# Sums of 32 steps' outputs on TensorE by products with the identity, and GpSimd in the recurrence from pair 53

## The chip, the core and the metric

One core of a Trainium2 chip. The metric is the device time of one launch in microseconds; three runs of the kernel before gave 1234.92, 1235.33 and 1239.51 us.

## What is computed

A layer norm of x (8 x 512 x 256) feeds two branches, a recurrent attention and a mixture of experts, whose product is added to x:

```python
def step(S, inp):                      # 512 steps; S is [batch, head, 16, 16], 8 batches x 16 heads
    qt, kt, vt, at, gkt = inp
    S = S * jnp.exp(gkt)[..., None]
    sab = jnp.einsum('bhk,bhkv->bhv', at, S)
    S = S + kt[..., None] * (sab[..., None, :] + vt[..., None, :])
    ot = jnp.einsum('bhk,bhkv->bhv', qt, S)
    return (S, ot)
...
xn = _layernorm(x, axis=-1)
s = attention(xn)                      # the recurrence, its output gated, normed and times Wo
g = _silu(experts(xn))                 # 8 experts, the 2 best of each token, gelu, layer norm
x = x + s * g
```

## The kernel before

**Layout.** The 128 pairs of batch and head are the 128 partitions, so a state is 16 x 16 values on each partition, and the 512 steps are done one after the other, two at a time. The program calls two steps g a pair; there are 256 pairs (g from 0 to 255), eight to a chunk (NP = 8), 32 chunks. Each chunk's records (decay, key, query, value, output gate, the a of the reference) are in memory as one block of 768 KB and are loaded by SyncE into one of three buffers of rbh; the load of chunk c + 3 waits for the gating of chunk c.

**Stages.** First TensorE projects 32 tiles of tokens and VectorE turns them into records, woven into pairs 0 to 28. At pair 29 VectorE does the routing. GpSimd then issues 64 scatters (L499) that sort the tokens by expert, and when all have landed ScalarE loads the first sorted rows (L698). Then TensorE and ScalarE run 39 expert tiles of 256 rows each: turn the rows (L875), first product (L887), gelu (L708), second product in two halves (L899, with the bias in L901), scaling of each half by ScalarE (L719). Last, the expert outputs are loaded, added, normed, and multiplied with the attention's output; this stage is woven into the recurrence from pair 224 (WOVEN = 28 chunks) and needs GpSimd's spreads (L533 to L538).

**One pair on VectorE alone.** Up to pair 55 `two_steps` does all on VectorE: products of the state with a (L1167), the decayed state (L1170), sums (L1172), the new state (L1190, L1196), and the reading of outputs. Reading is a product with q over 16 x 16 values (`read_left` L318 for the state that the pair before left, `read_found` L323 for the state in the middle) written to prod_q, with a 17th column, and a sum over the 17 columns (`sum_row`, L1156) two pairs later, into obh. Output row r is 2g - 1 + side. Every 16 rows are multiplied by the output gate (`gate_outputs`, L300) at the fourth pair (GATED = 3) of the next chunk.

**One pair shared.** From pair 56 (chunk SHARED = 7) `two_shared_steps` leaves the big products to GpSimd (`products`: L312 for a and decay, L329 for the reading; L318 and L323 at the first pair of a chunk), with a and two small tiles in PSUM. VectorE keeps the sums, the outer products and the state (L1206 to L1227). GpSimd's program for these pairs is one list in order: the products of a pair, then, at fixed pairs, the landing of an expert tile's half (`land`, L527, an indirect DMA that waits for ScalarE's scaled half), the numbering of the next tile (`number`, L517), gating and preparation of chunks, and from pair 224 the outputs' work. The pairs for landings come from a plan: landing of tile t's first half when (g - 56) x 3.83 + 390 is at least 390 + 15.9 t. An engine executes its instructions in order, so what waits holds back all behind it.

**Order of the names.** s_chain counts VectorE's steps in a pair (nine each), s_q the readings, s_o the summed rows, s_og the gated chunks, s_ys the scaled halves. TensorE's expert part starts with `turn_rows(0, 0, 0)`, which waits for the first sorted rows. The region `work` holds records first and expert tiles later.

## Time and profile before

| | |
|---|---|
| median of three runs | 1235.33 us |
| the profiled execution | 1241.86 us, span 1240.1 us |
| busy: TensorE, VectorE, GpSimd, ScalarE | 76%, 90%, 75%, 32% |
| pairs on VectorE alone, with tiles | 0 to 28 |
| routing | about 240 to 260 us |
| scatters on GpSimd | 260 to 362 us |
| first expert tile on TensorE | 366 us |
| pair 56, first with GpSimd | 391 us |
| last expert tile's end | 1003 us |

The page gives busy time by engine, the chain of work that ended last, and groups of instructions by line. The timeline gives start and duration of each instruction and, in brackets, how long its engine was idle before it and what ended that. VectorE's instructions overlap a little at their ends, so the distance between two starts says more than a duration.

### The profile page before, as it was taken

To read this page: it belongs to the slowest core of one execution; us is meant where nothing else is said; L and a number is where in the kernel's file an instruction comes from. 1 tells how busy PE (TensorE), PEld (TensorE's weight loads), DVE (VectorE), ACT (ScalarE), POOL (GpSimd) and SP (SyncE) were. 2 spreads that over 40 slices of the span, in tenths; PEclk is the share of its full clock that TensorE was granted. 3 is DMA by queue.
4 is the path that set the end of the run, shared out by engine and by line. 5 is a ranking of instruction groups with operands and counts; after the bars stand their busy time and mean duration, and the time that the engine had idled before them with its cause. 6 is when DMAs were issued, how large, how long until landed. Compare 5 with 4: busy or idle time off the path is not lost.

```text
span 1240.1 us, 17339 instructions
## 1 busy us (share of the span) xinstructions
PE 941.8 (76%) x3773; PEld 686.6 (55%) x3774; DVE 1122.2 (90%) x3478; ACT 398.0 (32%) x1015; POOL 933.0 (75%) x926
## 2 busy tenths in 40 slices
PE   5888888200019999999999999999999952667663
PEld 2333333100017778888787878887888841445442
DVE  3789999999999999999999999899999999978882
ACT  3444544200003232233223333332332213454552
POOL 3766666447753888888888888888888888777763
PEclk9788989655559999999999999999999985676777
DMA  5565655464333566666566666666666453443322
GB/s 163 171 226 178 188 201 190 147 211 114 108 107 119 174 190 200 195 199 189 181 188 192 199 201 185 185 192 199 199 199 192 131 150 101 111 135 117 83 68 56
DMA packets 238034, 202.59 MB, mean 163 GB/s; under 512 B 140401, under 2 KB 216017, under 8 KB 237969
## 3 DMA queue, kind: packets, MB, share of 16 engines
q1 hardware_dynamic: 160930, 82.81, 25.5%
q10 hardware_dynamic: 70224, 100.49, 24.4%
q0 software_dynamic: 6816, 18.69, 4.5%
q14 instruction: 54, 0.44, 0.1%
q8 instruction: 10, 0.16, 0.1%
HBM read 139.42 MB, written 62.54 MB: 163 GB/s over the span
## 4 chain that ended last, share of the span: by engine, by line
PE 56%; DVE 17%; POOL 8%; DMA 7%; issue 6%; ACT 4%; SPq 3%; ACTq 0%; DVEq 0%; POOLq 0%
PE psF L899 22%; PE psA L887 20%; POOL xs_d L499 6%; PE psA L955 4%; PE psF L901 4%; DMA rec_d<-work 3%; PE psF L917 2%; DMA work<-xs_d 2%; DVE obh L1156 2%; SPq L337 2%; DVE ubuf L1172 1%; PE psT L875 1%; DVE prod_a L1167 1%; DVE work L1009 1%; PE psT L949 1%
## 5 line engine op out<-in xcount | busy, mean ns | idle before, releaser
L312 POOL TENSOR_TENSOR prod_a<-state,rbh 128x512 f32<-128x512 f32 x200 | 254.4, 1272 | 94.0 <-DVE state L1227 68.8
L899 PE MATMUL psF<-wts,work 128*128 128x256 f32 x1248 | 290.0, 386 | 2.3 <-ACT work L708 1.2
L887 PE MATMUL psA<-xT,wts 128*128 128x256 f32 x1248 | 281.9, 385 | 1.3 <-ACT xT L702 0.8
L887 PEld LDWEIGHTS psA<-xT,wts 128*128 128x128 f32 x1248 | 235.6, 191 | 45.0 <-issue 13.8
L899 PEld LDWEIGHTS psF<-wts,work 128*128 128x128 f32 x1248 | 232.3, 191 | 48.1 <-issue 16.8
L329 POOL TENSOR_TENSOR prod_q<-state,rbh 128x512 f32<-128x512 f32 x175 | 221.9, 1268 | 0.0
L1156 DVE TENSOR_REDUCE obh<-prod_q 128x16 f32<-128x272 f32 x512 | 218.7, 428 | 0.0
L708 ACT ACTIVATE work<-psA,b_sb 128x256 f32<-128x256 f32 x312 | 130.7, 470 | 162.4 <-PE psA L887 159.0
L1214 DVE TENSOR_REDUCE ubuf<-prod_a 128x16 f32<-128x272 f32 x200 | 86.1, 431 | 46.5 <-POOL prod_a L312 46.4
L719 ACT ACTIVATE work<-psF,work 128x256 f32<-128x256 f32 x78 | 36.9, 473 | 256.8 <-PE psF L901 245.7
L875 PE MATMUL psT<-ident,work 128*128 128x128 f32 x156 | 24.2, 279 | 118.2 <-DMA work<-xs_d 118.2
L481 POOL TENSOR_TENSOR rinv<-ssm,neghalf 128x16 f32<-128x16 f32 x32 | 100.7, 3148 | 2.7
L499 POOL DMA_INDIRECT xs_d<-x_acc,idx x64 | 79.0, 1234 | 19.5 <-issue 18.9
L527 POOL DMA_INDIRECT y_d<-work,ids x78 | 78.9, 1011 | 14.6 <-issue 12.6
L1227 DVE TENSOR_TENSOR state<-psB,outer 128x256 f32<-128x256 f32 x200 | 84.4, 422 | 5.8
L1206 DVE TENSOR_TENSOR prod_a<-state,psT 128x256 f32<-128x256 f32 x200 | 83.9, 420 | 6.0
L875 PEld LDWEIGHTS psT<-ident,work 128*128 128x128 f32 x156 | 19.3, 143 | 123.9 <-issue 115.3
L1209 DVE TENSOR_REDUCE psB<-prod_a 128x16 f32<-128x272 f32 x200 | 86.8, 434 | 0.0
L1220 DVE TENSOR_TENSOR psB<-prod_a,psB 128x256 f32<-128x256 f32 x200 | 83.8, 419 | 0.0
L1212 DVE TENSOR_TENSOR psB<-rbh,psB 128x256 f32<-128x256 f32 x200 | 83.7, 419 | 0.0
L1222 DVE TENSOR_TENSOR outer<-rbh,psB 128x256 f32<-128x256 f32 x200 | 83.0, 415 | 0.0
L841 PE MATMUL psA<-w_kq,xT 128*128 128x512 f32 x128 | 78.9, 749 | 0.0
(171 smaller groups left out, 1564.0 us busy)
## 6 DMA issues: line engine op xcount, KB each, us to landing
wts<-in_L_ffn_W_dram ACTq DMA_DIRECT2D x78, 1024.0 KB, 5.4
rec_d<-work SPq DMA_DIRECT2D x32, 768.0 KB
rbh<-rec_d SPq DMA_DIRECT2D x32, 768.0 KB, 5.6
xs_d<-zero SPq DMA_DIRECT2D x26, 387.0 KB, 9.2
work<-xs_d ACTq DMA_DIRECT2D x39, 258.0 KB, 5.6
wts<-y_d ACTq DMA_DIRECT2D x16, 512.0 KB, 5.7
x_acc<-in_L_attn_x_dram SPq DMA_DIRECT2D x32, 128.0 KB
o_d<-obh SPq DMA_DIRECT2D x32, 128.0 KB, 7.3
```

Of the source, the lines that this page charges most:

```text
L312: eng.tensor_tensor(prod_a[:, n, 1:3, :, 0:HD], state[:, g % SR, :, :].unsqueeze(1).broadcast_to(wide), rows.unsqueeze(2).broadcast_to(wid ...
L329: eng.tensor_tensor(prod_q[:, g % SR, :, :, 0:HD], state[:, g % SR, :, :].unsqueeze(1).broadcast_to(wide), rbh[:, u, 2 * n - 1:2 * n + 1, ...
L481: pool.tensor_tensor(rinv[:, u, :], ssm[:, u, :], neghalf[:, 0:H], ALU.pow).then_inc(s_ng, 1)
L499: pool.indirect_dma_start(xs_d, bass.IndirectOffsetOnAxis(idx[:, 2 * n + c:2 * n + c + 1], 0), x_acc[:, n, :], None).then_inc(s_sc, 16)
L708: act.activation(hT[:, m, :], psA[m // 2 % 2][:, m % 2 * MT:(m % 2 + 1) * MT], ACT.Gelu, bias=b1_sb[:, bass.ds(e * FC + m, 1)]).then_inc(s ...
L887: mm = pe.matmul(psA[m // 2 % 2][:, m % 2 * MT:(m % 2 + 1) * MT], w1_sb[v][:, c, m * P:(m + 1) * P], xgT[:, c, :], start=(c == 0), stop=(c ...
L899: pe.matmul(psF[q][:, 0:D], hT[:, m, q * P:(q + 1) * P], w2_sb[v][:, m, :], start=(m == 0), stop=False)
L1156: dve.tensor_reduce(obh[:, c % OB, row % RING, :], prod_q[:, g % SR, side, :, :], AX.X, ALU.add).then_inc(s_o, 1)
L1206: dve.tensor_tensor(prod_a[:, n, 0, :, 0:HD], old, over_v(home_a[:, n, :]), ALU.mult).then_inc(s_chain, 1)
L1209: dve.tensor_reduce(u1, prod_a[:, n, 0, :, :], AX.X, ALU.add).then_inc(s_chain, 1)
L1214: dve.tensor_reduce(raw, prod_a[:, n, 2, :, :], AX.X, ALU.add).then_inc(s_chain, 1)
L1227: dve.tensor_tensor(new, home_o, outer[:, 1, :, :], ALU.add).then_inc(s_chain, 1)
```

## The change

Five things are changed together.

1. For pairs 32 to 47 the readings go to a ring of 16 rows, `q_rows`, in the upper part of `work` (the records there are done by then), and VectorE's sums of rows 64 to 94 are left out. Instead TensorE adds the 17 columns of eight rows at a time in PSUM: 17 products of the identity with one column of each row (128 columns with a step of 17 elements), in four groups of four pairs. VectorE fills the padding column once at pair 32 and waits for the groups (s_ro) before it uses ring rows again.
2. The gating of chunks 4 and 5 reads PSUM and moves from the fourth to the seventh pair (LATER = 6) of the next chunk: pairs 46 and 54. A last row of chunk 5 is gated by an instruction of its own. The gating of chunk 6, at pair 59, stays.
3. In pairs 34 to 49 `read_found` moves behind the new state, to where the sum stood.
4. GpSimd joins at pair 53 (SWITCH) in place of 56. It no longer waits for its scatters' completion (ScalarE still does), numbers tile 0 behind pair 56 and lands tile 0's first half at pair 57 in place of 56. Chunk 6's preparation also copies a to PSUM.
5. TensorE does the four groups ahead of its expert tiles, and waits for the gating of chunk 5, at pair 54, before it touches the first tile, because both use the same PSUM bank.

```diff
--- before.py
+++ after.py
@@ -46,7 +46,11 @@
 SR = 4
 RB = 3
 GATED = 3
+LATER = 6
 SHARED = 7
+SWITCH = 53
+SUMS = 32, 48
+SUMMED = range(2 * SUMS[0], 2 * SUMS[1] - 1)
 LAND0, LAND_STEP = 390.0, 15.9
 PAIR_STEP = 3.83
 
@@ -162,9 +166,12 @@
         psT = [ps(f"psT{n}", [P, 512]) for n in range(2)]
         sums = [psF[0], psF[1]]
         home_a = psT[1][:, 0:NP * HD].rearrange("p (n k) -> p n k", n=NP)
+
+        q_sums = psF[0][:, :].rearrange("p (r v) -> p r v", v=HD)
         home_u = psB[1][:, 0:4 * HD].rearrange("p (r j v) -> p r j v", r=2, j=2)
         home_o = psB[1][:, 4 * HD:4 * HD + HD * HD].rearrange("p (v k) -> p v k", v=HD)
 
+        q_rows = work[:, 32 * D - RING * HD * ROW:32 * D].rearrange("p (r v k) -> p r v k", r=RING, v=HD)
         oTs = xTs
         sel = gw[:, 0, :, :].rearrange("p t e -> p (t e)")
         b2_flat = b2_sb[:, :, :].rearrange("a e n -> a (e n)")
@@ -247,6 +254,7 @@
         s_dec = sem("s_dec")
         s_q = sem("s_q")
         s_pad = sem("s_pad")
+        s_ro = sem("s_ro")
         s_o = sem("s_o")
         s_og = sem("s_og")
         s_od = [sem(f"s_od{n}") for n in range(OB)]
@@ -291,14 +299,31 @@
 
         def prepared(c):
 
-            return 8 * min(c + 1, SHARED + 1) + (c >= SHARED) + 3 * max(0, c - SHARED)
+            return 8 * min(c + 1, SHARED + 1) + (c >= SHARED - 1) + (c >= SHARED) + 3 * max(0, c - SHARED)
 
         def shared(g):
-            return g // NP >= SHARED
+            return g >= SWITCH
+
+        def read_rows(g):
+
+            if SUMS[0] <= g < SUMS[1]:
+                return q_rows[:, 2 * g % RING:2 * g % RING + 2, :, :]
+            return prod_q[:, g % SR, :, :, :]
+
+        def summed(row):
+
+            return row + 1 - max(0, min(row + 1 - SUMMED.start, len(SUMMED)))
 
         def gate_outputs(eng, c):
-            eng.tensor_tensor(obh[:, c % OB, :, :], obh[:, c % OB, :, :], rbh[:, c % RB, :, O_:O_ + HD], ALU.mult)\
-                .then_inc(s_og, 1)
+            given = max(0, min(RING, SUMMED.stop - c * RING)) if SUMMED.start <= c * RING else 0
+            if given > 0:
+                at = c * RING - 2 * SUMS[0] + 1
+                ins = eng.tensor_tensor(obh[:, c % OB, 0:given, :], q_sums[:, at:at + given, :],
+                                        rbh[:, c % RB, 0:given, O_:O_ + HD], ALU.mult)
+            if given < RING:
+                ins = eng.tensor_tensor(obh[:, c % OB, given:, :], obh[:, c % OB, given:, :],
+                                        rbh[:, c % RB, given:, O_:O_ + HD], ALU.mult)
+            ins.then_inc(s_og, 1)
 
         def over_v(row):
             return row.unsqueeze(1).broadcast_to([P, HD, HD])
@@ -315,12 +340,12 @@
 
         def read_left(eng, g):
             n, u = (g - 1) % NP, (g - 1) // NP % RB
-            eng.tensor_tensor(prod_q[:, g % SR, 0, :, 0:HD], state[:, g % SR, :, :],
+            eng.tensor_tensor(read_rows(g)[:, 0, :, 0:HD], state[:, g % SR, :, :],
                               over_v(rbh[:, u, 2 * n + 1, Q_:Q_ + HD]), ALU.mult).then_inc(s_q, 1)
 
         def read_found(eng, g):
             n, u = g % NP, g // NP % RB
-            eng.tensor_tensor(prod_q[:, g % SR, 1, :, 0:HD], state[:, g % SR, :, :],
+            eng.tensor_tensor(read_rows(g)[:, 1, :, 0:HD], state[:, g % SR, :, :],
                               over_v(rbh[:, u, 2 * n, Q_:Q_ + HD]), ALU.mult).then_inc(s_q, 1)
 
         def read_both(eng, g):
@@ -507,7 +532,6 @@
             pool.wait_ge(s_idx, 3)
             for n in range(NT):
                 scatter(n, 1)
-            pool.wait_ge(s_sc, 32 * NT)
 
             def number(t):
                 v = t % 2
@@ -540,12 +564,14 @@
             def products(g):
                 c, n = g // NP, g % NP
                 pool.wait_ge(s_chain, g * CHAIN + 1)
+                if g == SWITCH:
+                    pool.wait_ge(s_prep, prepared(c))
                 if n == 0 and c == SHARED:
                     pool.wait_ge(s_prep, prepared(c))
                 if n == 0 and c > SHARED:
                     pool.wait_ge(s_pp, 3 * (c - SHARED))
                 decay_and_read(pool, g)
-                pool.wait_ge(s_o, 2 * (g - SR) + 1)
+                pool.wait_ge(s_o, summed(2 * (g - SR)))
                 if n == 0:
                     read_left(pool, g)
                     read_found(pool, g)
@@ -584,12 +610,13 @@
                     pool.wait_ge(s_pp, done + 2)
                     pool.tensor_tensor(fk, fk, both(REC + F_), ALU.mult).then_inc(s_pp, 1)
 
-            number(0)
             landed = 0
-            for g in range(SHARED * NP, T // 2):
+            for g in range(SWITCH, T // 2):
                 products(g)
+                if g == SHARED * NP:
+                    number(0)
                 ready = LAND0 + landed // MH * LAND_STEP
-                if landed < NM * MH and (g - SHARED * NP) * PAIR_STEP + LAND0 >= ready or g >= WOVEN * NP - 1:
+                if landed < NM * MH and g > SHARED * NP and (g - SHARED * NP) * PAIR_STEP + LAND0 >= ready or g >= WOVEN * NP - 1:
                     while landed < NM * MH:
                         t, q = divmod(landed, MH)
                         land(t, q)
@@ -599,9 +626,9 @@
                         if g < WOVEN * NP - 1:
                             break
                 if g % NP == GATED and g // NP > SHARED:
-                    pool.wait_ge(s_o, g // NP * RING)
+                    pool.wait_ge(s_o, summed(g // NP * RING - 1))
                     gate_outputs(pool, g // NP - 1)
-                if 4 <= g % NP < 7 and g // NP + 1 < NCH:
+                if 4 <= g % NP < 7 and SHARED < g // NP + 1 < NCH:
                     prepare_part(g // NP + 1, g % NP - 4)
                 s = g - WOVEN * NP
                 if s >= 0:
@@ -901,6 +928,20 @@
                     pe.matmul(psF[q][:, 0:D], ones[0:1, :], b2_flat[:, bass.ds(e * D, D)], start=False, stop=True)\
                         .then_inc(s_y, 1)
 
+
+            for m in range(SUMS[0] // 4, SUMS[1] // 4):
+                at = (4 * m - SUMS[0]) * 2
+                pe.wait_ge(s_chain, (4 * m + 4) * CHAIN + 1)
+                pe.wait_ge(s_q, 2 * (4 * m + 3) + 1)
+                for c in range(SHARED - 1):
+                    if SUMS[0] < (c + 1) * NP and (c + 1) * NP + LATER < 4 * m + 4 and SUMMED.stop > c * RING:
+                        pe.wait_ge(s_og, c + 1)
+                for k in range(ROW):
+                    mm = pe.matmul(q_sums[:, at:at + NP, :], ident[:, :], q_rows[:, 8 * m % RING:8 * m % RING + NP, :, k],
+                                   start=(k == 0), stop=(k == ROW - 1))
+                mm.then_inc(s_ro, 1)
+            pe.wait_ge(s_og, (SUMMED.stop - 1) // RING + 1)
+
             turn_rows(0, 0, 0)
             with pe.Fori(0, (NM - 1) // 2) as tp:
                 for v in range(2):
@@ -1129,7 +1170,7 @@
                 dve.tensor_reduce(pair[:, :, :], cross[:, :, :, :], AX.X, ALU.add).then_inc(s_prep, 1)
                 dve.wait_ge(s_prep, first + 6)
                 dve.tensor_tensor(f1, f1, f2_, ALU.mult).then_inc(s_prep, 1)
-                if c >= SHARED:
+                if c >= SHARED - 1:
                     dve.tensor_copy(home_a, a1).then_inc(s_prep, 1)
                 dve.wait_ge(s_prep, prepared(c))
 
@@ -1148,12 +1189,14 @@
             def sum_row(g, side):
 
                 row = 2 * g - 1 + side
+                if row in SUMMED:
+                    return
                 c = row // RING
                 dve.wait_ge(s_q, min(2 * g + 1, T))
                 dve.wait_ge(s_chain, min(g + 1, T // 2) * CHAIN)
                 if row % RING == 0 and c >= OB:
                     dve.wait_ge(s_od[c % OB], c // OB * 16)
-                dve.tensor_reduce(obh[:, c % OB, row % RING, :], prod_q[:, g % SR, side, :, :], AX.X, ALU.add).then_inc(s_o, 1)
+                dve.tensor_reduce(obh[:, c % OB, row % RING, :], read_rows(g)[:, side, :, :], AX.X, ALU.add).then_inc(s_o, 1)
 
             def two_steps(g, tile=None):
                 n, u, par = g % NP, g // NP % RB, g % 2
@@ -1168,6 +1211,8 @@
                                   rbh[:, u, 2 * n:2 * n + 2, A_:A_ + HD].unsqueeze(2).broadcast_to([P, 2, HD, HD]),
                                   ALU.mult).then_inc(s_chain, 1)
                 dve.tensor_tensor(decayed, old, over_v(rbh[:, u, 2 * n, F_:F_ + HD]), ALU.mult).then_inc(s_dec, 1)
+                if SUMS[0] + NP <= g < SUMS[1] and g % 4 == 0:
+                    dve.wait_ge(s_ro, (g - NP - SUMS[0]) // 4 + 1)
                 dve.wait_ge(s_chain, done + 1)
                 dve.tensor_reduce(ubuf[:, par, :, :], prod_a[:, n, 0:3:2, :, :], AX.X, ALU.add).then_inc(s_chain, 1)
                 if g > 0:
@@ -1188,12 +1233,15 @@
                 dve.wait_ge(s_chain, done + 4)
                 dve.wait_ge(s_dec, g + 1)
                 dve.tensor_tensor(decayed, decayed, outer[:, 0, :, :], ALU.add).then_inc(s_chain, 1)
-                read_found(dve, g)
-                dve.tensor_scalar(prod_q[:, g % SR, 1, :, HD], u1, pair[:, 0, n:n + 1], None, ALU.mult).then_inc(s_chain, 1)
+                if g - 2 not in range(*SUMS):
+                    read_found(dve, g)
+                dve.tensor_scalar(read_rows(g)[:, 1, :, HD], u1, pair[:, 0, n:n + 1], None, ALU.mult).then_inc(s_chain, 1)
                 if tile is not None:
                     scale_a(tile - 1)
                 dve.wait_ge(s_chain, done + 6)
                 dve.tensor_tensor(new, decayed, outer[:, 1, :, :], ALU.add).then_inc(s_chain, 2)
+                if g - 2 in range(*SUMS):
+                    read_found(dve, g)
                 if g > 1:
                     sum_row(g - 2, 1)
 
@@ -1233,7 +1281,7 @@
 
             def chunk(c, u, slots=None, outs=None):
                 dve.wait_ge(s_rb[u], c // RB * 16 + 16)
-                if c == SHARED:
+                if c == SHARED - 1:
                     dve.wait_ge(s_v, NT)
                     dve.wait_ge(s_gam, NT)
                 if c <= SHARED:
@@ -1243,9 +1291,16 @@
                 for n in range(NP):
                     if slots is not None and slots + n == NT + 1:
                         route()
-                    if n == GATED and 0 < c <= SHARED:
-                        dve.wait_ge(s_o, c * RING)
+                    if 0 < c <= SHARED and n == (LATER if (c - 1) * RING in SUMMED else GATED):
+                        dve.wait_ge(s_o, summed(c * RING - 1))
+                        if (c - 1) * RING in SUMMED:
+                            dve.wait_ge(s_ro, (min(c * RING, SUMMED.stop) - SUMMED.start) // NP + 1)
                         gate_outputs(dve, c - 1)
+                    if c * NP + n == SUMS[0]:
+                        for r in range(RS):
+                            dve.wait_ge(s_recd[r], 16 * (NT // RS))
+                        dve.memset(q_rows[:, 0::2, :, HD], 0.0).then_inc(s_pad, 1)
+                        dve.wait_ge(s_pad, SR + 1)
                     if shared(c * NP + n):
                         two_shared_steps(c * NP + n, outs + n if outs is not None else None)
                     else:
@@ -1275,7 +1330,7 @@
                 for side in range(2):
                     sum_row(g, side)
             sum_row(T // 2, 0)
-            dve.wait_ge(s_o, NCH * RING)
+            dve.wait_ge(s_o, summed(NCH * RING - 1))
             gate_outputs(dve, NCH - 1)
 
             for n in range((NCH - WOVEN) * NP - LAG, NT - 1):
```

## Rows read from the trace of the kernel before

**Rows 1.** The page: busy time by engine, chain that ended last, chunk loads.

```profile
PE 941.8 (76%) x3773; PEld 686.6 (55%) x3774; DVE 1122.2 (90%) x3478; ACT 398.0 (32%) x1015; POOL 933.0 (75%) x926
...
PE 56%; DVE 17%; POOL 8%; DMA 7%; issue 6%; ACT 4%; SPq 3%; ACTq 0%; DVEq 0%; POOLq 0%
...
rbh<-rec_d SPq DMA_DIRECT2D x32, 768.0 KB, 5.6
```

**Rows 2.** Timeline, TensorE: start, duration, work, [idle before, its end].

```profile
366.11 1.09 PE L875 MATMUL psT<-ident,work 128*128 128x128 f32 x4 [114.60 <-DMA work<-xs_d]
```

**Rows 3.** Windows: length; busy PE, PEld, DVE, ACT, POOL; PEclk, DMA, GB/s.

```profile
391.00:1005.00 614.00, 606.65 (x2713) 490.56 (x2711) 578.35 (x1818) 183.95 (x414) 540.33 (x534) 1.00 0.62 186
```

**Rows 4.** Timeline of ScalarE, behind the expert stage.

```profile
1039.07 1.02 ACT L772 ACTIVATE wts<-psF,ysh,yrs 128x256 f32<-128x256 f32 x2 [19.89 <-POOL ysh L538]
```

**Rows 5.** Timelines of ScalarE and GpSimd: results and landings, tiles 0 and 38.

```profile
382.32 0.47 ACT L719 ACTIVATE work<-psF,work 128x256 f32<-128x256 f32 x1 [2.55 <-PE psF L901]
...
394.04 1.01 POOL L527 DMA_INDIRECT y_d<-work,ids  x1 [0.15 <-issue]
...
999.26 0.47 ACT L719 ACTIVATE work<-psF,work 128x256 f32<-128x256 f32 x1 [3.14 <-PE psF L901]
...
1000.80 1.01 POOL L527 DMA_INDIRECT y_d<-work,ids  x1 [0.16 <-issue]
```

**Rows 6.** Timeline of GpSimd, a landing in between.

```profile
782.38 1.02 POOL L527 DMA_INDIRECT y_d<-work,ids  x1 [1.41 <-issue]
```

**Rows 7.** Timeline of VectorE, a pair that it does alone.

```profile
264.25 0.68 DVE L1167 TENSOR_TENSOR prod_a<-state,rbh 128x512 f32<-128x512 f32 x1
...
268.79 0.69 DVE L1167 TENSOR_TENSOR prod_a<-state,rbh 128x512 f32<-128x512 f32 x1
...
270.68 0.43 DVE L1156 TENSOR_REDUCE obh<-prod_q 128x16 f32<-128x272 f32 x1
271.03 0.23 DVE L1178 SCALAR_TENSOR_TENSOR ubuf<-ubuf,pair 128x16 f32<-128x16 f32 x1
```

**Rows 8.** Timeline of VectorE, padding columns filled at the start.

```profile
48.36 0.15 DVE L1267 MEMSET prod_q<- 128x16 f32 x4
```

**Rows 9.** Timeline of VectorE: pair 53; chunk 7 prepared; pairs 56 and 57.

```profile
375.43 0.69 DVE L1167 TENSOR_TENSOR prod_a<-state,rbh 128x512 f32<-128x512 f32 x1
...
389.05 0.30 DVE L1122 TENSOR_TENSOR cross<-rbh 128x128 f32<-128x128 f32 x1
...
390.79 0.31 DVE L1133 COPY psT<-rbh 128x128 f32<-128x128 f32 x1
391.13 0.42 DVE L1206 TENSOR_TENSOR prod_a<-state,psT 128x256 f32<-128x256 f32 x1
...
394.69 0.42 DVE L1206 TENSOR_TENSOR prod_a<-state,psT 128x256 f32<-128x256 f32 x1
```

**Rows 10.** Timeline of GpSimd, the last scatter.

```profile
360.35 1.22 POOL L499 DMA_INDIRECT xs_d<-x_acc,idx  x1 [0.30 <-issue]
```

**Rows 11.** Timeline of TensorE: tile 0, its transposes; four transposes later.

```profile
367.95 5.56 PE L887 MATMUL psA<-xT,wts 128*128 128x256 f32 x16 [0.76 <-ACT xT L702]
374.04 3.72 PE L887 MATMUL psA<-xT,wts 128*128 128x256 f32 x16 [0.53 <-ACT work L708]
377.60 0.60 PE L875 MATMUL psT<-ident,work 128*128 128x128 f32 x4
...
1044.49 1.11 PE L939 MATMUL psB<-ident,gT 128*128 128x128 f32 x4 [3.23 <-ACT gT L780]
```

**Rows 12.** Timeline of queues and TensorE around tile 2's wait for rows.

```profile
402.42 0.36 SPq L371 DMA_DIRECT2D rbh<-rec_d  x1
...
403.04 0.69 ACTq L698 DMA_DIRECT2D work<-xs_d  x1
...
412.23 0.73 PE L875 MATMUL psT<-ident,work 128*128 128x128 f32 x4 [2.67 <-DMA work<-xs_d]
...
413.18 5.14 PE L899 MATMUL psF<-wts,work 128*128 128x256 f32 x16 [0.23 <-issue]
```

## What the change does to the time, predicted

> **What bounds the kernel now.** I read the page first, then the waits, then the order of time around the two places where engines meet. VectorE is busy for 90% of the span and TensorE for 76% [rows 1], which reads like a kernel bound by VectorE. The chain that ended last says something else: 56% of it is TensorE and 17% VectorE [rows 1]. The stages explain it. Up to 366.11 us TensorE has been idle for 114.60 us [rows 2], while VectorE works and GpSimd issues scatters. From 391 to 1005 us TensorE is busy for 606.65 of 614 us at full clock: this is the expert stage, 39 tiles [rows 3]. After it TensorE and ScalarE wait again, for 19.89 us, until GpSimd's spread of the first outputs, which its list of work puts at pair 224 of the recurrence [rows 4].
>
> So two tracks run beside each other: the expert tiles (TensorE, ScalarE) and the recurrence (VectorE, GpSimd). They are tied by GpSimd's landings of tile results (line 527), which stand at fixed pairs in its program and wait for ScalarE's scaled result (line 719). I compared the two for the same tile. Tile 0: result done at 382.79 us, landing at 394.04, so 11.1 us in hand (less the 0.15 us of issue). Tile 38, the last: 999.73 and 1000.80, so 0.9 us [rows 5]. In between GpSimd already waits for a tile here and there, 1.41 us at 782.38 [rows 6]. That is the main reading: at the start the recurrence is the later of the two, at the end they are level. A recurrence that comes earlier buys at most 0.9 us at tile 38 unless the tiles come earlier too.
>
> **The change part by part, in time of the profiled execution.** It ran 1241.86 us with a span of 1240.1; the three timed runs have a median of 1235.33, so this profile is 6.5 us above it. I add what I find to both.
>
> *The removed sums.* 31 rows (64 to 94) lose their VectorE sum. One sum takes 0.43 us but its neighbour starts 0.35 us after it (270.68 to 271.03) [rows 7], 0.34 elsewhere; with 0.345 that is 31 x 0.345 = 10.7 us. A pair of 4.54 us (264.25 to 268.79) becomes 3.86. The product of line 323 moves behind the new state, where the sum stood, so an instruction of about the same length still lies between the state and its first reader; I cost the move at nothing. Were that cover gone, a pair would wait for up to those 0.34 us and the sum would have saved nothing.
>
> *Small additions on VectorE.* One memset of the padding with its wait: the nearest row is four memsets of 128x16 in 0.15 us each [rows 8]; bounds 0.1 and 0.6 us, I take 0.3. The wait beside it is for the last records in memory; the program finishes them at pair 28, four pairs and the routing earlier, and a transfer of the same 768 KB lands in 5.6 us [rows 1], so it costs nothing. The copy of line 1133 now also in chunk 6: 0.34 us (390.79 to 391.13) [rows 9]. The gate of chunk 4 only moves; that of chunk 5 moves behind pair 53, so 0.34 us less ahead of it.
>
> *GpSimd from pair 53.* Pair 53 starts at 375.43 now [rows 9], so after the change at 375.43 - 10.7 + 0.3 + 0.34 - 0.34 = 365.0 us. The last scatter is issued at 360.35 for 1.22 us [rows 10], so GpSimd is free, by 3.5 us. Shared pairs start 3.56 us apart when nothing is added (391.13 to 394.69) [rows 9], against 4.54: 3.0 us gained over three pairs. The gate at pair 54, in two parts, costs 0.34 + 0.2, of which 0.34 was there before. Chunk 7 is prepared at 376.2 instead of 389.05 [rows 9]: **the recurrence leads by 12.8 us** when the expert stage begins.
>
> *TensorE's sums.* Four groups of 17 products with 128 columns; in float32 each shows as two instructions (32 for a tile's 16 calls), so 34 a group. The trace shows no product with a moving operand that takes every 17th element. The nearest rows are four transposes of 128 columns: 1.11 us at 1044.49, in a stretch of low clock, and 0.60 at full clock (377.60) [rows 11]; less the first one's fill that is 0.25 and 0.11 us an instruction. A group costs 8.5 us or 3.8 us. After idling, tile 0 ran 16 instructions in 5.56 us and the next 16 in 3.72 [rows 11], so the clock should rise inside a group: about 22 instructions in 5.5 us and 12 in 1.3, 6.8 us. I take 6.8. It is hidden as long as a group ends before its reader: the third group can start at pair 44 and its reader, the gate of chunk 4, stands at pair 46, two pairs or 7.7 us later, 7.5 with the signals. The ring of rows needs a group only every four pairs, 15.4 us.
>
> *The new wait ahead of the tiles.* This is the term that decides. TensorE now waits for the gate of chunk 5, at pair 54: 365.0 + 3.56 = 368.5, plus 0.6 for the gate: 369.2 us. Before, it started at 366.11, when the first rows had landed [rows 2]. Queued behind this wait is everything TensorE has: all 39 tiles. **Tiles start 3.1 us later.** Bounds: 0 if the pairs shrink by more than I think, 5 if the groups run at low clock throughout and the copies or waits cost their upper ends.
>
> *Moved numbering and landing.* The first numbering goes behind pair 56, about 382 us; the load that needs it is issued behind tile 0's second half, after its first half's result at 386, so it is hidden. The first landing goes from pair 56 to 57, one pair of 3.7 us later. SP's loads of chunks 7 and 8 follow gates that come at pairs 46 and 54: needed at 56 and 60, they have about 37 and 22 us for a load of 5.6 us [rows 1].
>
> *Sum.* Relative to the tiles the recurrence is now 12.8 + 3.1 = 15.9 us earlier, 12.2 at tile 0. Tile 0 had 11.1 in hand: GpSimd waits 1 us there already, and as the hand falls to 0.9 us at tile 38 it waits 15.0 us in all. The products of the recurrence stand behind each such wait, so the lead is given back. Tile 38 lands at its result, 3.1 us later than now, which was 0.9 before its landing: +2.2 us. After it nothing changes. Span 1240.1 + 2.2 = 1242.3; against the median, 1235.33 + 2.2, **1237.5 us**.
>
> **The rivals.** *R1, the tiles also speed up.* In tile 2 TensorE waited 2.67 us for the next rows, whose load was issued at 403.04, 0.6 us after SP's chunk load of 402.42; its next 16 products then took 5.14 us [rows 12], where 16 take 3.72 at full clock [rows 11]: 4.1 us lost. The phase between gates and tiles changes, so this may go: 1237.5 - 4.1 = 1233.4, and down to 1229 if smaller delays go too. Against it: chunks and tiles differ in length, drift through each other in any case and meet elsewhere.
>
> *R2, the landings don't hold the recurrence.* If it keeps its 12.8 us to pair 224, the time is 1222.5. For it: ScalarE stands ready for 19.89 us there [rows 4]. Against: [rows 5, 6].
>
> *R3, slower: a group outlasts its reader.* If a group takes 15 us (34 x 0.44, a strided operand that costs nearly twice the 0.25 us, for which there is no row), the gate at pair 46 waits 15.0 - 7.5 = 7.5 us, the gate at 54 moves by as much and with it all tiles: 1237.5 + 7.5 = 1245.0. It decides from 7.5 us a group on. The Trainium skill speaks for it ("SBUF - State Buffer", section "Door 1: The DMA port swizzle"): float32 reads stepping over more than four elements leave the 16-byte line each time and pay. By that rule the group would be the long one; no row of this trace shows such an operand on TensorE, and the page gives no size.
>
> *R4, the freed VectorE time is lost.* If taking a sum out uncovers waits, a pair stays at 4.2 us instead of 3.86, tiles start 5.4 us later still: 1242.9. Against: each waiting instruction has one independent instruction left ahead of it.
>
> **How the numbers follow.** Forecast 0.50 (its own range 1234 to 1241, from the bounds 0 and 5 of the start and the spread of the three runs), R1 0.22, R2 0.07, R3 0.12, R4 0.09. This kernel's runs can tell about 0.5%, 6.2 us: faster means below 1229.2, slower above 1241.5. Faster: R2 and a third of R1 with everything small gone, 0.15. Slower: R3, two thirds of R4 and the upper tail of the forecast, 0.21. The same: 0.64. The range 1229 to 1245 leaves out R2, the part of R1 below 1229 and about half of R3, 0.19 in all.
>
> **What would show it.** Right: pairs 36 to 48 about 3.86 us apart; TensorE's first transpose of rows near 369.2 us, right behind line 300's second part; landings with waits ahead of them that sum to about 15 us; the last landing about 3 us later than its result now. Wrong: first tile at or before 366 (then +2.2 becomes -0.9), groups on TensorE longer than 7.5 us, landings that follow pairs rather than results, or a stretch from the first to the last tile that differs from now by more than 2 us, which moves everything behind it.

## Result: 2% slower, and the profile after

The changed kernel takes 1261.77 us (median of four runs, 1261.2 to 1262.31), the kernel before 1235.12 on the same chip: ratio 1.02 [1.018, 1.0219]. The forecast was 1237.5 with a range of 1229 to 1245. One run of the kernel before that took 2013.68 us, on a chip of the experiments (chip 0), stands outside all ratios below. The profiled run took 1261.2 us with a span of 1259.5; below, times of before are those of its own profile, span 1240.1.

The page of the changed kernel: busy time by engine, share of the chain that ended last, scatters as a group (count, busy us, mean ns, idle before).

```profile
PE 968.5 (77%) x3909; PEld 713.2 (57%) x3910; DVE 1109.4 (88%) x3444; ACT 397.9 (32%) x1015; POOL 930.0 (74%) x932
...
PE 47%; DVE 27%; POOL 7%; issue 7%; ACT 4%; DMA 3%; another core or an unknown queue 2%; SPq 1%; ACTq 0%; DVEq 0%; POOLq 0%
...
L524 POOL DMA_INDIRECT xs_d<-x_acc,idx x64 | 69.8, 1090 | 19.5 <-issue 18.9 <-POOL idx L520 0.3 <-POOL x_acc L531 0.3
```

VectorE is busy 12.8 us less than in [rows 1] (31 sums at 0.43 us are 13.3), so the work did leave it, and the kernel is slower all the same. The new entry in the chain is "another core or an unknown queue", 2% or some 22 us. One core runs, so it is a wait whose releaser the profile doesn't know. The waits (engine, line, waited for: total, times, longest) and the timeline of VectorE name it:

```profile
DVE obh L321 <- remote: 21.9, 1, 21.9
```

```profile
329.66 0.69 DVE L1210 TENSOR_TENSOR prod_a<-state,rbh 128x512 f32<-128x512 f32 x1
...
333.24 0.42 DVE L348 TENSOR_TENSOR work<-state,rbh 128x256 f32<-128x256 f32 x1
355.56 0.42 DVE L321 TENSOR_TENSOR obh<-psF,rbh 128x256 f32<-128x256 f32 x1 [21.89 <-remote]
```

The waiting instruction is the gate of chunk 4 at pair 46. Between 333.66 and 355.56 us VectorE does nothing. It waits for the third group of TensorE's sums (s_ro at 3). TensorE's timeline has the four groups and the first expert tile:

```profile
292.66 8.03 PE L940 MATMUL psF<-work,ident 128*128 128x128 f32 x34 [41.86 <-DVE work L348]
308.33 8.02 PE L940 MATMUL psF<-work,ident 128*128 128x128 f32 x34 [7.64 <-DVE work L348]
325.98 8.03 PE L940 MATMUL psF<-work,ident 128*128 128x128 f32 x34 [9.62 <-DVE work L348]
363.92 8.02 PE L940 MATMUL psF<-work,ident 128*128 128x128 f32 x34 [29.91 <-DVE work L348]
392.21 1.12 PE L902 MATMUL psT<-ident,work 128*128 128x128 f32 x4 [20.27 <-DVE obh L324]
```

The third group ends at 334.01, yet its reader starts at 355.56. The trace also keeps records of semaphore increments, which no view lists. For s_ro these are:

| group | last product ends | increment recorded | late by |
|---|---|---|---|
| 1 | 300.69 | 308.88 | 8.2 us |
| 2 | 316.35 | 316.37 | 0.0 |
| 3 | 334.01 | 355.46 | 21.5 |
| 4 | 371.94 | 371.95 | 0.0 |

Group 1's delay costs nothing: its first reader, pair 40, starts at 310.08, and so the record alone shows this delay. Group 3's stops VectorE. Of all of TensorE's increments in the trace of before, none comes over 0.3 us after its product. The last scatter is issued at 350.49 and has landed by 352.76; the late increment follows 2.7 us on.

From there everything shifts. The first tile starts at 392.21 instead of 366.11 [rows 2], +26.1 us, behind the gate of chunk 5. Results and landings of tiles 0 and 38, from the timelines of ScalarE and GpSimd:

```profile
408.46 0.47 ACT L746 ACTIVATE work<-psF,work 128x256 f32<-128x256 f32 x1 [2.56 <-PE psF L928]
...
409.71 1.02 POOL L551 DMA_INDIRECT y_d<-work,ids  x1 [2.47 <-DVE obh L1199]
...
1022.78 0.47 ACT L746 ACTIVATE work<-psF,work 128x256 f32<-128x256 f32 x1 [3.14 <-PE psF L928]
...
1024.04 1.01 POOL L551 DMA_INDIRECT y_d<-work,ids  x1 [0.18 <-issue]
```

Against [rows 5]: tile 0's landing follows its result by 0.8 us instead of 11.3, tile 38's by 0.8 as against 1.1. From the first of these results to the last it takes 614.3 us (616.9 before), and from tile 38's result to the end 236.3 us (1023.25 to 1259.5; before 999.73 to 1240.1, 240.4). So +26.1 at the start, -2.6 in the tiles and -4.1 behind them give the span's +19.4. Among the kernels below that are on time the same distances lie between 617 and 626 us and between 234 and 241. So the -4.1 is within what these kernels vary by; the -2.6 comes from a distance of 614.3 that lies below all of them, and what made it isn't shown.

### The profile page after: what moved, and what is told of

Same layout as the page of the kernel before. It is cut to its first block, busy times and chain, and to the rows that moved or that the text cites. A ratio compares the mean times of both kernels' runs of the same rounds, so it can differ in the third digit from the quotient of the medians.

```text
span 1259.5 us, 17559 instructions
## 1 busy us (share of the span) xinstructions
PE 968.5 (77%) x3909; PEld 713.2 (57%) x3910; DVE 1109.4 (88%) x3444; ACT 397.9 (32%) x1015; POOL 930.0 (74%) x932
## 4 chain that ended last, share of the span: by engine, by line
PE 47%; DVE 27%; POOL 7%; issue 7%; ACT 4%; DMA 3%; another core or an unknown queue 2%; SPq 1%; ACTq 0%; DVEq 0%; POOLq 0%
PE psF L926 18%; PE psA L914 17%; PE psA L996 4%; PE psF L928 3%; DVE ubuf L1217 3%; DVE obh L1199 3%; DVE prod_a L1210 2%; PE psF L958 2%; POOL prod_a L337 2%; POOL prod_q L354 2%; DVE state L1242 1%; DVE prod_a L1235 1%; DVE work L1050 1%; DMA work<-xs_d 1%
## 5 line engine op out<-in xcount | busy, mean ns | idle before, releaser
L337 POOL TENSOR_TENSOR prod_a<-state,rbh 128x512 f32<-128x512 f32 x203 | 258.0, 1271 | 111.3 <-DVE state L1275 71.2
L354 POOL TENSOR_TENSOR prod_q<-state,rbh 128x512 f32<-128x512 f32 x178 | 225.7, 1268 | 0.0
L1199 DVE TENSOR_REDUCE obh<-prod_q 128x16 f32<-128x272 f32 x480 | 205.3, 428 | 0.0
L940 PE MATMUL psF<-work,ident 128*128 128x128 f32 x136 | 32.1, 410 | 89.0 <-DVE work L348 89.0
L524 POOL DMA_INDIRECT xs_d<-x_acc,idx x64 | 69.8, 1090 | 19.5 <-issue 18.9
L940 PEld LDWEIGHTS psF<-work,ident 128*128 128x128 f32 x136 | 29.7, 275 | 91.7 <-DVE state L1242 48.4
L729 ACT ACTIVATE xT<-psT 128x512 f32<-128x512 f32 x39 | 23.3, 597 | 171.2 <-PE psT L902 152.7
```

Source lines behind the costliest of these rows:

```text
L337: eng.tensor_tensor(prod_a[:, n, 1:3, :, 0:HD], state[:, g % SR, :, :].unsqueeze(1).broadcast_to(wide), rows.unsqueeze(2).broadcast_to(wid ...
L354: eng.tensor_tensor(prod_q[:, g % SR, :, :, 0:HD], state[:, g % SR, :, :].unsqueeze(1).broadcast_to(wide), rbh[:, u, 2 * n - 1:2 * n + 1, ...
L1199: dve.tensor_reduce(obh[:, c % OB, row % RING, :], read_rows(g)[:, side, :, :], AX.X, ALU.add).then_inc(s_o, 1)
```

## Experiments

Chips are told here because they turned out to matter. "Late" is the time from a group's last product to its increment.

**What holds the third increment?** My theory A was that TensorE's increment stays until TensorE has something else to do (it idles 29.91 us ahead of group 4). Theory B blamed the halves of the ring or of the bank. Four kernels on one chip (chip 11; before 1239.56 us, 13 runs).

Two more products, into a bank that nothing uses, behind each group:

```diff
                 mm.then_inc(s_ro, 1)
+                for k in range(2):
+                    pe.matmul(psA[0][:, 0:P], ident[:, :], ident[:, :], start=True, stop=True)
```

> The changed kernel with two products of the identity with itself (no wait, into an unused PSUM bank) behind the last product of each group. In the changed kernel the increments of groups 1 and 3 came 8.2 and 21.5 us after their last product ended, those of groups 2 and 4 at once. Theory A (the increment is held while TensorE has nothing to do behind it): all four come on time, the gate of chunk 4 waits under 1.5 us, tiles start near 371 us, total near 1240 us. Theory B (it belongs to the half of the ring that a group reads) and theory C (GpSimd's scatters hold it): nothing changes, gate near 355.5, tiles at 392 us, total near 1262 us.

Measured: 1265.47 us, 1.02 [1.0158, 1.0243]. TensorE's timeline shows the products running at once behind group 3, and VectorE still waits:

```profile
334.49 0.63 PE L944 MATMUL psA<-ident 128*128 128x128 f32 x4
```

```profile
DVE obh L321 <- remote: 20.9, 1, 20.9
```

The increment is 20.4 us late (the one of group 1 has no record in this trace). TensorE works on in order while its increment is missing, so A falls.

The halves of the ring exchanged:

```diff
-                return q_rows[:, 2 * g % RING:2 * g % RING + 2, :, :]
+                at = (2 * g + NP) % RING
+                return q_rows[:, at:at + 2, :, :]
...
-  q_rows[:, 8 * m % RING:8 * m % RING + NP, :, k]
+  q_rows[:, (8 * m + NP) % RING:(8 * m + NP) % RING + NP, :, k]
```

> The changed kernel with the two halves of the ring exchanged, so groups 1 and 3 read rows 8 to 15 and groups 2 and 4 rows 0 to 7. Theory B (half of the ring): groups 2 and 4 become the late ones and the gate of chunk 4 waits under 1.5 us; total near 1240 unless group 4 is later than pair 54. Theories A and C: the same groups 1 and 3 are late, gate near 355.5 us, total near 1262 us.

Measured: 1268.42 us (one run). Groups 1 and 3 are late again, by 3.8 and 18.4 us, groups 2 and 4 aren't. VectorE's timeline:

```profile
351.98 0.42 DVE L322 TENSOR_TENSOR obh<-psF,rbh 128x256 f32<-128x256 f32 x1 [18.84 <-remote]
```

It is not a matter of which half of the ring; B falls for the ring.

Only GpSimd's earlier join, without the sums:

```diff
-SUMS = 32, 48
+SUMS = 32, 32
```

> The changed kernel with no pairs summed on TensorE: only GpSimd's earlier join and what goes with it. The prediction's reasoning (the landings hold the recurrence to the tiles): tiles start at 366 us as before, the recurrence leads by 3 us, of which at most 0.9 us is kept: 1234 to 1236 us. Rival (the join costs by itself, by contention with the scatters' end or the tiles' first loads): 1240 us or more.

Measured: 1244.55 us, 1.0038 [1.0019, 1.0058]. No wait for s_ro, the first tile at 368.3, and a cost of 0.4% (5.0 us between the medians) where I expected none. Of it 2.2 us lie in the later first tile: the last scatter is issued at 362.44 instead of 360.35 [rows 10]. Its tiles take 621.2 us from first to last result, 616.9 in before, which is within what the other kernels vary by; so the rest is not placed.

Only the sums, GpSimd joining at pair 56 as before (the preparation of chunk 6 put back as well):

```diff
-SWITCH = 53
+SWITCH = 56
```

> The changed kernel with GpSimd joining at pair 56 as before: only the sums on TensorE. If the loss lies with the sums: gate of chunk 4 near 355.5 us, tiles at 392 to 393 us, total 1261 to 1264 us. If the join has a part in it: clearly less than 1261 us.

Measured: 1265.61 us, 1.0202 [1.015, 1.0254]; group 3 late by 20.2 us. The 2% come with the sums; the earlier join isn't needed for them.

**Is it the scatters?** In the changed kernel and the three with sums the third increment came 0.7 to 2.7 us after the last scatter had landed (355.46 after 352.76, 351.88 after 351.16, 354.35 after 351.68, 355.11 after 353.74). The next four kernels went to chip 15 (before: one run, 1239.18 us). A pause of GpSimd between its two sets of scatters, so that group 3 ends with none under way:

```diff
+            for n in range(56):
+                pool.memset(zero[:, :], 0.0).then_inc(s_pz, 1)
+                pool.wait_ge(s_pz, n + 1)
             for n in range(NT):
                 scatter(n, 1)
```

> The changed kernel with 56 memsets of an unused tile on GpSimd between its two sets of scatters, about 40 us in which no scatter is issued; group 3 of TensorE's sums ends in it. In the four runs so far the late increment of group 3 came 0.7 to 2.7 us after the last scatter had completed. Theory C (the scatters hold it): group 3's increment comes within 0.5 us of its last product, and the gate of chunk 4 waits under 1.5 us; the tiles start late for another reason, the second set's end near 385 to 390 us. Theory D (it has nothing to do with them, for example a fixed place in the program or in PSUM): 18 to 22 us late as before.

The increment carried by a product of its own:

```diff
+                mm = pe.matmul(psA[0][:, 0:P], ident[:, :], ident[:, :], start=True, stop=True)
                 mm.then_inc(s_ro, 1)
```

> The changed kernel with one product of the identity with itself, into an unused PSUM bank, behind each group, which carries the group's increment in place of the group's last product. If only the signal of a product that reads ring rows and writes the sums' bank is late: on time, total near 1240 us. If any increment of TensorE at this moment is held: group 3 about 20 us late, total near 1262 us.

The sums in another PSUM bank:

```diff
-        q_sums = psF[0][:, :].rearrange("p (r v) -> p r v", v=HD)
+        q_sums = psA[0][:, :].rearrange("p (r v) -> p r v", v=HD)
```

> The changed kernel with the sums in the bank of psA0 in place of psF0. Theory E (the bank or the columns in it hold the last product): on time, near 1240 us. Theory C: as before, gate near 355 us, near 1262 us.

The ring laid out so that TensorE's moving operand comes in runs of 16 neighbouring elements and VectorE's writes step (the product then reads `q_cols[..., k, :]`):

```diff
-        q_rows = work[...].rearrange("p (r v k) -> p r v k", r=RING, v=HD)
+        q_cols = work[...].rearrange("p (r k v) -> p r k v", r=RING, v=HD)
+        q_rows = q_cols.rearrange("p r k v -> p r v k")
```

> The changed kernel with a ring row laid out column by column, so that each of TensorE's 17 products reads runs of 16 neighbouring elements instead of every 17th. If the step in the moving operand sets the group's 8.0 us: a group of 4 to 7 us. If it is the weight load or the clock: 8.0 us. VectorE's product that writes with a step of 16 may take longer than 0.42 us. Theory C on the increment: late as before, total near 1262 us; if the strided product is what is late: near 1238 us.

Measured, in that order: 1276.58, 1245.4, 1241.41 and 1250.54 us. In all four every increment came on time. The pause's 1276.58 is its own price: it holds the first tile until 401.9. In bankA the wait at pair 46 and those of the landings are (DVE, then POOL):

```profile
DVE obh L321 <- PE psA L940: 0.4, 1, 0.4
```

```profile
POOL y_d L551 <- ACT work L746: 16.4, 10, 4.7
...
POOL y_d L551 <- DVE obh L1199: 2.5, 1, 2.5
```

It looked as though four different edits each cured it, which is too good: either all of them touch the cause, or the chip does.

For the groups' length kmajor tells something else. TensorE's timeline:

```profile
293.73 5.58 PE L941 MATMUL psF<-work,ident 128*128 128x128 f32 x34 [42.67 <-DVE work L349]
310.06 5.93 PE L941 MATMUL psF<-work,ident 128*128 128x128 f32 x34 [10.75 <-DVE work L349]
```

The same 34 instructions take 5.4 to 5.9 us with runs of 16 elements and 8.0 with the step of 17. The clock doesn't explain it: the mean granted clock of the four groups is 0.66 to 0.74 here and 0.65 to 0.74 in the changed kernel. VectorE's products into the ring, the groups by shape, rise from 0.42 to 0.58 us and more:

```profile
L349 DVE TENSOR_TENSOR work<-state,rbh 128x256 f32<-128x256 f32 x16 | 9.4, 587 | 0.0
L344 DVE TENSOR_TENSOR work<-state,rbh 128x256 f32<-128x256 f32 x16 | 9.2, 578 | 0.0
```

The time that TensorE saved was hidden, the time that VectorE lost wasn't: the first tile starts at 373.13 instead of bankA's 370.59. (The times of the two, one run each, can't be compared so finely: bankA's kernel, timed ten times as bankA3 below, ranges from 1244.8 to 1255.35.)

The banks again, on chip 0 (before 1245.76 us, 19 runs), with psF's other bank, with the 128-column parts of the bank exchanged in pairs, and with a bank that no tile needs, so that the tiles needn't wait for chunk 5's gate:

> The same kernel as the one with the sums in the bank of psA0, now timed. In its one look all four increments were on time, tiles started at 370.6 us and it took 1241.41 us beside 1239.18 for the kernel before. If the late increment was avoided by the bank: every execution about 2 us (0.1 to 0.4%) slower than before, as the prediction's sum of +2.2 us has it. If it was avoided by chance: some executions near 1262 us.

```diff
-        q_sums = psF[0][:, :].rearrange("p (r v) -> p r v", v=HD)
+        q_sums = psB[0][:, :].rearrange("p (r v) -> p r v", v=HD)
...
-            pe.wait_ge(s_og, (SUMMED.stop - 1) // RING + 1)      # ahead of the tiles
+            pe.wait_ge(s_og, (SUMMED.stop - 1) // RING + 1)      # behind them, ahead of the outputs' work
```

> The changed kernel with the sums in the bank of psB0, which the expert tiles don't use, and so without the wait for the gate of chunk 5 ahead of the first tile. The prediction's reasoning: tiles start near 366 us as before, the recurrence leads by about 12 us and gives back all but the 0.9 us that it had in hand at tile 38: 1 us faster than before to 1 us slower, and 3 to 5 us faster than with psA0. Rival R2 (the landings don't hold the recurrence): 10 us or more faster than before.

```diff
-        q_sums = psF[0][:, :].rearrange("p (r v) -> p r v", v=HD)
+        q_sums = psF[1][:, :].rearrange("p (r v) -> p r v", v=HD)
```

> The changed kernel with the sums in the bank of psF1 in place of psF0. If something about psF0 alone (or a coincidence in time) makes the increment late: on time, near 1242 us. If it is the bank's last user (the projection's second low-rank product, which used psF0 and psF1 alike): late as in the changed kernel, near 1262 us.

```diff
-                    mm = pe.matmul(q_sums[:, at:at + NP, :], ident[:, :], ...
+                    mm = pe.matmul(q_sums[:, at ^ NP:(at ^ NP) + NP, :], ident[:, :], ...
```

> The changed kernel, bank psF0, with the 128-column parts of the bank exchanged in pairs: groups 1 and 3 write columns 128 to 255 and 384 to 511, groups 2 and 4 columns 0 to 127 and 256 to 383. The gates take three and two more instructions of VectorE, about 0.5 us. If the columns decide: group 2 late and 3 on time, near 1243 us. If it is the place in time: group 3 late again, near 1262 us.

Measured: bankA3 1250.1 us, 1.0027 [1.0006, 1.0047]; bankB 1242.77, 0.9972 [0.9954, 0.9991]; bankF1 1248.46 and swapcols 1248.94, one run each. Again all increments on time, also in the bank of the changed kernel. BankB beats bankA3 by 7.3 us, where I expected 3 to 5, and before by 3.0 us between the medians, where I expected 1 at most. Its first tile doesn't start near 366 us but 8 us earlier, on the load of its rows:

```profile
358.55 1.12 PE L902 MATMUL psT<-ident,work 128*128 128x128 f32 x4 [7.62 <-DMA work<-xs_d]
```

**Is it the chip?** Seven different kernels without the delay on two chips, three with it on chip 11 (and the changed kernel's first result, whose chip isn't known). So the changed kernel unaltered, and three of the "cures", went back to chip 11 (before 1243.97, 3 runs).

> The changed kernel unaltered, as the control. Theory F (an edit of the program, such as another bank, decides): group 3's increment about 20 us late and 1.9 to 2.2% slower than before. Theory G (the late increment belongs to the chip or its state and not to the edit): on time, tiles at 371 to 372 us, 0.1 to 0.5% slower than before, as with the sums in psA0.

> The kernel with GpSimd's 40 us of memsets between its two sets of scatters, again. Theory C (scatters under way hold the increment): on time while after_ctl is late. Theory G: the same as after_ctl, late or on time. Total near 1275 us if on time, for the scatters' sake.

> The kernel whose group increments are carried by a product of its own behind each group, again. If the product that carries the increment decides: on time while after_ctl is late, near 1243 us. Theory G: the same as after_ctl.

> The kernel with the sums in the bank of psF1, again. If the bank of psF0 decides: on time while after_ctl is late, near 1243 us. Theory G: the same as after_ctl.

| kernel on chip 11 | us | group 1 late | group 3 late |
|---|---|---|---|
| after_ctl (unaltered) | 1265.53 | 4.7 us | 21.5 us |
| incfill2 | 1265.83 | 6.5 | 20.2 |
| bankF1b | 1274.34 | 7.5 | 21.4 |
| pause2 | 1272.58 | 4.6 | on time |

Neither psF's other bank nor the carrier cures anything here: incfill and bankF1, on time on chips 15 and 0, are late on chip 11. The other kernels of chips 15 and 0 (psA0, psB0, the exchanged columns, kmajor) were not run on chip 11. The pause does cure it, in its one run, and only for the group it protects: group 1, which ends while the first set of scatters is still being issued, is late as ever, while group 3 ends at 335.86 with no scatter under way and its reader waits 0.28 us:

```profile
335.97 0.42 DVE L322 TENSOR_TENSOR obh<-psF,rbh 128x256 f32<-128x256 f32 x1 [0.28 <-PE psF L944]
```

**What else the records show.** Each of the 64 scatters ends with 16 increments of one semaphore, 1024 in all. The traces of before and of every kernel on chips 15, 0 and 4 keep 1023 or 1024 records of them. The seven traces with a late third increment keep only 468 to 540, pause2 keeps 675, and join53, on chip 11 but without the sums, 960. The records are missing around the late groups. In the changed kernel there are 39 where about 224 are due from 292 to 309 us (due is a third of the scatters' packets that finished then, which is 16 for each scatter), and 61 of about 336 from 326 to 356. From 312 to 322 us, where group 2 ends on time, there are 88 of about 112. VectorE's records have gaps too: of the 127 of its instructions with an increment that end from 290 to 334 us, 99 have one. Its pairs still follow each other in 3.92 us, and ScalarE's load of the first rows, which needs all 1024, is issued at 353.06. So what is missing is records and not increments. The late increment of TensorE thus stands in stretches in which increments of other senders were recorded with gaps as well. It is not shown which of the two makes the other, or whether both have one cause; nor is it tested whether taking the trace has a part in it.

Last, the unaltered kernel on a fourth chip (chip 4; before 1243.41, 13 runs), with a version of bankB meant for chips like 11: both gates of summed rows at pairs 52 and 54, behind the scatters.

> The changed kernel unaltered, as the control for the chip. On a chip like number 11: group 3's increment 20 to 22 us late, near 1262 us. On one like 15 or 0 (not yet seen with this very kernel): on time, tiles near 371 us, near 1243 us.

```diff
-                for c in range(SHARED - 1):
-                    ...
-                        pe.wait_ge(s_og, c + 1)
...
-                    if 0 < c <= SHARED and n == (LATER if (c - 1) * RING in SUMMED else GATED):
+                    due = {6 * NP + 4: 4, 6 * NP + LATER: 5}.get(c * NP + n)
+                    if due is None and n == GATED and 0 < c <= SHARED and (c - 1) * RING not in SUMMED:
+                        due = c - 1
+                    if due is not None:
```

> The sums in the bank of psB0, no wait ahead of the tiles, no wait of group 4 for a gate, and the gate of chunk 4 at pair 52, the one of chunk 5 at pair 54, both behind all four groups and behind the scatters. If the loss is only VectorE's wait for an increment that is late while scatters run: on either kind of chip no wait over 1 us at the gates, tiles start at 358 to 360 us, and the time is 0.1 to 0.5% below the kernel before. If the late increment follows the program in another way: a wait of several us at pair 52, or at pair 40 or 44 in the ring.

Measured: after_ctl2 1247.65 us (one run), gate52 1239.88, 0.9977 [0.9952, 1.0002]. The unaltered kernel has its increments on time on this chip:

```profile
334.85 0.42 DVE L321 TENSOR_TENSOR obh<-psF,rbh 128x256 f32<-128x256 f32 x1 [0.45 <-PE psF L940]
```

In gate52 VectorE waits at neither gate (no idle time over 0.2 us from 290 to 385 us), and the first tile starts at 356.45, 1.5 us ahead of the earliest that I expected. Its ratio lies where I expected it, but its interval reaches 1.

The same program thus costs 1.8% on chip 11 (after_ctl, 1.0183 [1.0099, 1.0267], two runs; 2% in the first result) and about 0.3% on chip 4 (1247.65 against 1243.41, one run inside a spread of 1237.54 to 1250.44). gate52 was never run on chip 11, so whether it holds there is open.

**What is shown and what isn't.** Shown: the loss is one late increment of TensorE, of 18 to 22 us. It came in 6 of 6 profiled runs on chip 11 in which group 3 ended among scatters, and in none of 9 such runs on chips 15, 0 and 4; on chip 11, taking the scatters away from it removed it, in one run. Not settled: by what way an increment is held while scatters run, why group 2, which ends 6.6 us into the second set, is on time in every run, and what sets chip 11 apart. "Held until the last scatter is done" fits group 3 alone: in halves, late56 and after_ctl group 1's increment is recorded 0.2 to 0.6 us before the last scatter of the first set is even issued. VectorE's steps and TensorE's products run on at their pace.

## Why the prediction was wrong, step by step

*The step that failed.* "It is hidden as long as a group ends before its reader: ... two pairs or 7.7 us later, 7.5 with the signals." The 0.2 us for a signal was taken for granted; it was 21.5. The sum has nothing for a wait at pair 46; VectorE waited 21.89 us there, and the tiles started 26.1 us later instead of 3.1. R3 had the right shape (a group's result outlasts the gate at pair 46, and the gate at 54 with all tiles moves by as much), but named the products' length as the cause, 7.5 us of delay, and gave 1245.0. I had priced the work on both sides of the new wait and not the signal between them.

The Trainium skill's page "Perfetto Trace Analysis", section "Tensor Engine Instruction (MATMUL, LD_WEIGHTS)", says that a matmul's end in the profile is estimated, and that its semaphore update comes later, once PSUM has acknowledged the write. That order is what the table above shows for group 3 (334.01, then 355.46). It gives no reason for 21 us, and the filler's products, which started at 334.49, speak against the group itself having run on so long.

*Where increments were on time, the sum held.* bankA3 measured +0.27% [0.06, 0.47] against the predicted 2.2 us or 0.18%. Its terms, one by one:

- A pair without its sum: 3.92 us (321.83 to 325.75 in the changed kernel) against 3.86. Right; R4's 4.2 is out.
- A group: 8.03 us instead of 6.8. The step of 17 costs: 34 instructions (two for each product) start 0.227 us apart, at either level of the clock. Two windows of group 1 (length; busy PE, PEld, DVE, ACT, POOL with counts; PEclk, DMA, GB/s) have 0.22 us for an instruction at a granted clock of 0.50 (1.2 GHz) and of 1.00 (2.4 GHz):

```profile
292.66:296.90 4.24, 4.24 (x19) 4.24 (x20) 4.24 (x12) 0.00 (x0) 3.08 (x4) 0.50 1.14 236
296.92:300.70 3.78, 3.77 (x17) 3.08 (x16) 3.78 (x12) 0.00 (x0) 2.90 (x3) 1.00 0.31 110
```

  So my mean of two clocks was the wrong working for this operand. The group outlasts the 7.5 us, which is R3's condition, by half a microsecond, and the gate waits 0.4 to 0.5 us. The Trainium skill's rule about lines of 16 bytes ("SBUF - State Buffer", section "Door 1: The DMA port swizzle") points the right way; the size, 8.03 us a group against 5.4 to 5.9, is from kmajor.
- Start of the tiles: 370.6 to 373.1 us in the on-time profiles with the pair-54 wait and no pause, against 369.2, with the gate as what ends TensorE's idle time. Right in kind, 1.4 us or more short.
- The lead given back: landings waited 16.4 + 2.5 us in bankA, against 15.0. Right, and R2, by which the lead would be kept, is out: in bankA tile 38's landing follows its result by 0.8 us, at 1006.8.
- R1: in the on-time profiles the distance from tile 0's result to tile 38's is 617 to 626 us, against 616.9 before. No gain there.

*A misread row.* [rows 6] was read as GpSimd waiting for a tile. The wait ends by "issue", at 782.38, while ScalarE's result was ready at 779.98. Before has 65 landings with such a wait, of 1.4 us at most, and none released by ScalarE. The tie showed only at tile 38 [rows 5]. The conclusion drawn from it held, not the row.

*A gain that I left out.* "The last scatter is issued at 360.35": I took the scatters as fixed. With VectorE's sums gone they go faster, 1090 ns each on average against 1234 before (the groups' lines; 79.0 us for the 64 in before), and the last is issued at 349 to 354 us. While VectorE stood still, each took 0.96 us. Join53, which leaves the sums on VectorE, has 1256 ns. So the first rows are there about 8 us earlier (358.55 in bankB against [rows 2]), and the shared bank's wait for chunk 5's gate costs 13.6 us (372.11 in bankA3, same chip), not the 3.1 that I set against 366.11. Here the change gives away, on a good chip too, the start that it gained: on chip 0 bankB, which keeps it, is 0.3% faster than before, and bankA3, which doesn't, 0.3% slower.

## What to carry to other kernels

A new wait between two engines has three prices: the work before it, the work behind it, and the delivery of the signal. Leave slack for the third, and most of all where GpSimd issues DMAs, or put the reader behind that stretch. And when an edit cures a delay, run the unaltered kernel beside it on the same chip before believing it: two "cures" here (the carrier, psF's other bank) were the chip, and the rest were never put to that test but for the pause, which passed. Borrow a buffer whose next user comes late (psB[0]) rather than the one that the next stage needs first (psF[0]).

## What the hardware showed beyond that

- TensorE's third group increment, on one of four chips known by number, came 18 to 22 us late while scatters were under way, with its products and VectorE's steps undisturbed. In the same traces 47 to 54% of the records of the scatters' increments are missing, and none or one of 1024 on the other three chips.
- GpSimd's issue of an indirect DMA depends on what VectorE does: its duration was 1.22 us at the median beside VectorE's full program (before), 0.99 beside the one without sums, 0.96 with VectorE idle (both in the changed kernel).
- One of the two instructions of a float32 product of 128 columns with a step of 17 elements took 0.22 to 0.23 us at either level of the clock; with runs of 16 elements it took 0.16 to 0.17, in stretches of mean clock 0.66 and 0.71.
- VectorE's product of 128x256 written with a step of 16 elements took 0.58 us instead of 0.42.
